# A Gram matrix matmul of 224 columns instead of 256, and one output matmul with an add behind it

## The reference

```
dots = jnp.einsum('bfd,bgd->bfg', bottom_output, bottom_output)
pairs = dots[:, _TRIL_I, _TRIL_J]
x = jnp.concatenate([bottom_mlp_output, pairs, pad], axis=1)     # 128 + 351 + 1
for w, b in ((w0, b0), (w1, b1), (w2, b2), (w3, b3)):            # 1024, 1024, 512, 256
    x = jax.nn.relu(x @ w.T + b)
return x @ w_out.T + b_out
```

## Time and profile before

| | |
|---|---|
| runs, median of three | 570.75 us |
| profiled execution, first to last instruction | 570.2 us |
| time of the profiled execution around its span | not given apart |
| TensorE busy, weight loads busy | 542.0 us (95%), 531.7 us (93%) |
| ScalarE busy | 340.8 us (60%) |
| VectorE busy | 330.0 us (58%) |
| matmuls of the whole program | 4457 |
| one chunk, from one output row to the next | 64.3 us |

### The profile page before, as it was taken

The page is one execution under the profiler, slowest core; times in us unless marked ns, Lnnn a source line. Parts: engine busy times, 40 slices in busy tenths (PEclk is TensorE's granted clock), DMA queues, the critical chain, the costliest instruction groups (busy, mean ns, idle before and its releaser), DMA issues.

```text
span 570.2 us, 13265 instructions
## 1 busy us (share of the span) xinstructions
PE 542.0 (95%) x4457; PEld 531.7 (93%) x4457; DVE 330.0 (58%) x941; ACT 340.8 (60%) x900; POOL 10.8 (2%) x58
## 2 busy tenths in 40 slices
PE   4768799999999999999999999999999999999997
PEld 3667799999999999999999999999999999999996
DVE  3778678727872488427872488427872488425222
ACT  4988479827971499317971499417981399414112
POOL 1500000000000000000000000000000000000000
PEclk9977899999999999999999999999999999999999
DMA  7987324044304141232304131222304131200000
GB/s 222 260 233 223 89 65 117 12 104 124 109 16 119 37 121 47 61 87 78 109 11 112 43 116 53 62 87 77 109 7 111 47 115 56 55 22 1 1 1 0
DMA packets 89898, 47.32 MB, mean 83 GB/s; under 512 B 25851, under 2 KB 88083, under 8 KB 89875
## 3 DMA queue, kind: packets, MB, share of 16 engines
q1 hardware_dynamic: 89874, 47.02, 29.5%
HBM read 41.03 MB, written 5.98 MB: 82 GB/s over the span
## 4 chain that ended last, share of the span: by engine, by line
PE 73%; ACT 12%; DMA 6%; issue 5%; SPq 2%; DVE 0%; ACTq 0%; DVEq 0%
PE acc L551 61%; ACT parts L641 9%; PE gram_ps L518 6%; PE turned_ps L502 5%; DMA rows<-in_r_bottom_output_dram 5%; ACT xt L624 2%; ACT h_full L654 1%; DMA blocks<-grams 1%; PE gram_ps L485 1%; SPq L366 1%; SPq L355 1%; SPq L344 1%; DMA pairs<-blocks 1%; PE turned_ps L564 0%; PE turned_ps L527 0%
## 5 line engine op out<-in xcount | busy, mean ns | idle before, releaser
L551 PE MATMUL acc<-h_a,w_hi 128*128 128x256 f32 x1152 | 211.2, 283 | 0.9 <-ACT h_full L654 0.8
L654 ACT ACTIVATE h_full<-acc,small_t 128x256 f32<-128x256 f32 x176 | 83.2, 473 | 183.2 <-PE acc L551 181.5
L551 PEld LDWEIGHTS acc<-h_a,w_hi 128*128 128x128 f32 x1152 | 179.2, 191 | 2.2 <-ACT h_full L654 2.2
L641 ACT ACTIVATE parts<-gram_ps 27x216 f32<-27x216 f32 x512 | 173.4, 339 | 5.9 <-PE gram_ps L518 1.1
L551 PE MATMUL acc<-h_a,w_lo 128*128 128x256 f32 x576 | 163.0, 283 | 0.0
L551 PEld LDWEIGHTS acc<-h_a,w_lo 128*128 128x128 f32 x576 | 110.4, 192 | 0.0
L551 PE MATMUL acc<-x,w_hi 128*128 128x256 f32 (+1 forms) x512 | 98.5, 289 | 3.7 <-DVE x L806 3.7
L518 PE MATMUL gram_ps<-xt 128*128 128x256 f32 x512 | 95.9, 312 | 1.0 <-ACT parts L641 0.7
L551 PE MATMUL acc<-h_b,w_hi 128*128 128x256 f32 x512 | 93.3, 284 | 0.0
L736 DVE TENSOR_TENSOR xt<-turned_ps,xt 128x432 fp32r<-128x432 f32 x128 | 77.3, 604 | 18.7 <-ACT xt L624 15.7
L502 PE MATMUL turned_ps<-ident,rows 108*128 108x108 f32 x512 | 72.8, 267 | 16.0 <-DMA rows<-in_r_bottom_output_dram 15.1
(11 more groups left out here) (54 smaller groups left out, 346.3 us busy)
## 6 DMA issues: line engine op xcount, KB each, us to landing
rows<-in_r_bottom_output_dram SPq DMA_DIRECT2D x128, 216.0 KB
blocks<-grams SPq DMA_DIRECT2D x32, 182.2 KB
stage_b<-in_L_rec_w_dram SPq DMA_DIRECT2D x2, 1024.0 KB, 9.6
stage_b<-in_L_rec_w_dram SPq DMA_DIRECT2D x1, 2048.0 KB, 7.8
stage_a<-in_L_rec_w_dram SPq DMA_DIRECT2D x1, 1536.0 KB, 11.5
stage_pairs<-in_L_rec_w_dram SPq DMA_DIRECT2D x1, 1408.0 KB, 9.7
mlp_rows<-r_bottom_mlp_output_dram SPq DMA_DIRECT2D x8, 128.0 KB, 2.2
pairs<-blocks SPq DMA_DIRECT2D x8, 126.0 KB
```

The source lines that it names most:

```text
L551: last = nc.tensor.matmul(acc_slot(slot), weight(wp, layer, m, k), in_tile(layer, k, xp), start=(k == 0 and n == 0), stop=(k == K_TILES[la ...
L641: last = nc.scalar.activation(parts[quad, u % 2, :, :, 0:FEATS], gram_ps[quad, b:b + GRAM_BANKS, :].rearrange("p a (b h n) -> p h (a b) n" ...
L654: nc.scalar.activation(h_full[:, slot % 2, :], acc_slot(slot), ACT.Relu, bias=small_t[:, slot:slot + 1]).then_inc(drained, 1)
```

## The change

The Gram matmul streams 28 columns of each sample (27 features and one zero), not 32: 224 columns. The stationary operand stays 128 columns wide. `xt` keeps its layout, so the moving operand is read in eight pieces of 28, and the results stand 28 apart in PSUM. ScalarE's copies L641 take them from there; their number and size stay.

The output row's two accumulating matmuls become one of 512 columns, high and low side by side in the whole bank. ScalarE reads the high half with the bias into `y_row` and gives a new semaphore, out_started. VectorE then adds the low half to `y_row` and gives out_drained.

```diff
+NARROW = 28
+HALF = GROUP * NARROW
...
-        out_bank = turned_ps[0:1, OUT_UNIT % TURN_RING, 0:CHUNK]
+        out_both = turned_ps[0:1, OUT_UNIT % TURN_RING, 0:2 * CHUNK]
+        out_high, out_low = out_both[:, 0:CHUNK], out_both[:, CHUNK:2 * CHUNK]
...
-                    last = nc.tensor.matmul(gram_ps[:, u % GRAM_RING * GRAM_BANKS + j // 2, at:at + 2 * P], xt[:, u % XT_RING, j, 0, :],
-                                            xt[:, u % XT_RING, j].rearrange("p h n -> p (h n)"), start=True, stop=True)
+                    last = nc.tensor.matmul(
+                        gram_ps[:, u % GRAM_RING * GRAM_BANKS + j // 2, at:at + 2 * HALF], xt[:, u % XT_RING, j, 0, :],
+                        xt[:, u % XT_RING, j].rearrange("p h (s f) -> p (h s) f", s=GROUP)[:, :, 0:NARROW],
+                        start=True, stop=True)
...
-                for part in range(2):
-                    last = nc.tensor.matmul(out_bank, ones[:], h_a[:, 4, part, :], start=(part == 0), stop=(part == 1))
-                last.then_inc(out_filled, 1)
+                nc.tensor.matmul(out_both, ones[:], h_a[:, 4].rearrange("p h n -> p (h n)"),
+                                 start=True, stop=True).then_inc(out_filled, 1)
...
-                        gram_ps[quad, b:b + GRAM_BANKS, :].rearrange("p a (b h n) -> p h (a b) n", h=2, n=P)[
-                            :, :, :, QUAD * s:QUAD * s + FEATS], ACT.Copy)
+                        gram_ps[quad, b:b + GRAM_BANKS, :].rearrange("p a (b x) -> p (a b) x", x=2 * P)[
+                            :, :, 0:2 * HALF].rearrange("p j (h n) -> p h j n", n=HALF)[
+                                :, :, :, NARROW * s:NARROW * s + FEATS], ACT.Copy)
...
-                nc.scalar.activation(by_sample(y_row[:, :]), cols(out_bank), ACT.Identity,
-                                     bias=bout[:, :]).then_inc(out_drained, 1)
+                nc.scalar.activation(by_sample(y_row[:, :]), cols(out_high), ACT.Identity,
+                                     bias=bout[:, :]).then_inc(out_started, 1)
...
+            def out_row(c):
+                dve.wait_ge(out_started, c + 1)
+                nc.vector.tensor_tensor(by_sample(y_row[:, :]), cols(out_low), by_sample(y_row[:, :]),
+                                        ALU.add).then_inc(out_drained, 1)
...
+                    elif step[0] == "out" and not (isinstance(c, int) and c == 0):
+                        out_row(c - 1)
...
             chunk(CHUNKS - 1)
+            out_row(CHUNKS - 1)
```

More of the change, by code:

```diff
@@ L284, in dlrm_program @@
         out_filled = sem("out_filled")
+        out_started = sem("out_started")
         out_drained = sem("out_drained")
```

## The result

The changed kernel is slower: 574.56 us in the median of 11 runs (572.83 to 576.73) against 570.75 (11 runs of the kernel before beside it, 569.37 to 572.54). The ratio is 1.0057 with a 95% interval of 1.0042 to 1.0072, so 3.3 us (2.4 to 4.1) are lost; it is not the quotient of the two medians, which lie 3.8 us apart. 574.6 was forecast.

A forecast was written before the change was run, and what follows sets the result against it. TensorE was taken to bound chunk 0, ScalarE's copies most of chunks 1 to 6. Add +4.3 in chunks, +0.7 at the end, Gram -1.1: +3.9 us, forecast 574.6 (572.9 to 576.2; with rivals A, B, C 571.6 to 577.2).

The forecast's parts named there:

- about level: Chunk 2: ScalarE needs 1.82 to 2.29 us a unit against 1.94 for TensorE, and started late.
- only units 14 and 15 come after: Chunks 1 to 6: only 8 Gram matmuls a chunk, behind ScalarE's path, save 10 ns each: 0.48 us in all.
- TensorE as the bound, so all 16 units: 0.64 us: Chunk 0: TensorE bounds, so all 64 Gram matmuls save 10 ns each, 0.64 us.
- At most 11 ns, I take 10: Saving per 224-column Gram matmul from a 120 ns period, limited by the next weight load of about 109 ns.
- D: VectorE add's time, taken as 0.68 us; also a rival: ScalarE not the path in chunks 1 to 6, 569.4, chance 0.08.
- rival B: Output row: the add is dear because its strided read pays too, +5.9 us, 576.6; chance 0.09.
- the 0.9 us: Sign: TensorE's six waits before unit 2's transposes are 0.9 us and name VectorE's new line.
- the other two stops: Sign: waits for h_full grow from 0.35 to about 0.65 us, those before Gram matmuls from 0.2 to about 0.45.
- 0.55 over that span: Whole kernel before: the runs' median, 570.75 us, lies 0.55 over the profiled span of 570.2.
- A: Output row rival: the add is cheap, 0.42 us, since one partition from PSUM hides the stride: 572.8; chance 0.15.
- C: Gram rival: no saving, since the load's handshake is the 120 ns: +5.0 us, 575.7; chance 0.11.
- E: Gram rival: under 256 columns each column costs more, 72 ns more per matmul, about 604 us; chance 0.07.

The follow-up runs named there:

- narrow: Kernel before with only the Gram matmul cut to 224 columns, output row as before: 569.55 us against 570.52, ratio 0.9996.
- narrow3: Kernel before with 224-column Gram matmuls and only three of four Gram copies per unit on ScalarE: 560.65 us, ratio 0.9827.
- wide3: Kernel before, 256 columns, but ScalarE makes only three of the four Gram copies of each unit: 563.72 us, ratio 0.9897.
- cols128: Kernel before with Gram matmuls streaming, and ScalarE copying, only the 128 columns of the high half: 561.9 us in one execution.
- flat: Changed kernel with y_row read and written at unit step by ScalarE and VectorE: 570.84 us in one execution.
- late_add: Changed kernel with the output row moved behind the chunk's last unit, out of its own buffer: 569.44 us, ratio 0.9986 to the kernel before.
- outrow: Kernel before with only the output row changed (one 512-column matmul and the VectorE add), Gram matmuls of 256 columns: 575.18 us, ratio 1.0096.

## Why the prediction was right, and where not

- **The bound.** Right for chunks 1 to 6: narrow lost all its saving but 0.03 us to ScalarE's row, narrow3 got 0.54. The two engines were not "about level", though: ScalarE's row of 28.58 us holds 14 rounds of copies, 2.04 us each with all that stands between them, against 1.94 for a unit on TensorE. But "only units 14 and 15 come after", 8 matmuls, was one unit too many: the copies that end near 228.5 are unit 13's, and four matmuls come after them. Wrong for chunk 0, "TensorE as the bound, so all 16 units: 0.64 us". From the first Gram matmul there to the first output matmul it is 53.16 us in both profiles of before, 52.91 and 52.84 after: 0.28 saved. With faster matmuls ScalarE became the path there too, and a new stop of 0.3 us stands before unit 15's Gram matmuls at 104.26; the 0.3 row in the list of waits is this one. With ScalarE's copies cut to three the same stretch goes from 53.16 (wide3) to 52.56 us (narrow3), 0.59 us less, so nearly all that was forecast comes there. A stage in which one engine is only just ahead of the other has room for a part of the gain.
- **Gram matmul.** "At most 11 ns, I take 10": 7 were measured, 119.0 to 112.1. The most frequent distances are 110 and 114, not 109. That the next load is the floor was right (cols128: 112 to 113 ns with 128 columns). The Trainium skill (TensorE: Matmul & The Clock Gate, Back-to-back issue gap) gives 96 ns for 224 columns by its formula, but states this for a single gap and says that in a stream of weight loads and matmuls both set the spacing; the trace agrees with the second and not with the 96.
- **The add.** D was put at 0.68 from the price of a strided write in L763; it was 0.60. Without the step it is 0.405 (0.416 was taken from L800), so the step costs 0.75 ns an element and not 1.08. Read and write in steps cost 0.19 us together, less than the 0.28 that the prediction has for the write by itself: rival B is out. The Trainium skill (SBUF — State Buffer, the note on SBUF cachelines) says that each access that crosses to a new 16-byte line pays; the 0.25 and 0.19 us of flat agree.
- **The path of the add.** As forecast: the stop grew by 0.64 in place of 0.71, six times, and ScalarE's idle time before its row by the same. VectorE had room. Of the signs, the 0.9 us came as 0.85, and the other two stops ("about 0.65" and "about 0.45") as 0.63 and 0.52. At the end of the program the add cost 0.63 (5.52 us from the last layer matmul against 4.89).
- **The sum.** From the two pairs of profiles: 6 x (64.94 - 64.32) = +3.7, -0.28 for chunk 0, +0.63 at the end: +4.0 us, against 3.8 between the medians and 3.3 (2.4 to 4.1) by the ratio. Forecast +3.9. That the forecast meets the median to 0.1 us is luck. Two errors went against each other: the seven stops were 0.07 to 0.08 too dear (0.5 us), and the Gram saving was put at 1.1 us where 0.28 + 6 x 0.03 = 0.5 came, so 0.6 us too much. With either alone the forecast would have been off by 0.5 to 0.6 us, still well inside its band of 572.9 to 576.2.
- **The base.** "0.55 over that span" was a coincidence of a long execution with the median; the true distance is 2.5 us. It did no harm, since the forecast added a difference to the median.
- **Rivals.** A (0.42) is what the add costs without its step, so it was the right number for another kernel. C was near for chunks 1 to 6, for another reason: the saving was there, ScalarE took it. D is out by narrow: ScalarE has no slack but is 0.10 us a unit behind, and only with three copies of four (wide3) does it idle, 0.4 us at a time. E is out: 224 columns take less than 256.

## What to carry to other kernels

Before an instruction is made shorter, ask of each stage which engine runs there without a hole. TensorE at 95%, with two stops of 0.2 to 0.35 us a chunk, was not the path among the units, and a saving of 6% on its Gram matmuls mostly lengthened the stops. A small add put between a result and the semaphore that frees its bank costs its whole length wherever the next writer of the bank already waits; the same add cost nothing inside a chunk where that writer comes well after it (late_add), so look for the place first. Compare repeating stages of two profiles, not their spans.

## What was not expected of the hardware

- A stream of fp32r matmuls with 256 columns starts every 120 ns, with weights of one column (L564) or of 128. With 224 columns, and with 128, most distances are 110 to 114 ns, and the weight loads start 109 to 113 ns apart.
- The waiting VectorE add started 0.09 us before the end of the instruction ahead of it (flat, 195.29 against 195.38).
- ScalarE's row of copies is 28.57 to 28.65 us long from one execution to another, alike in all chunks of one; the cause is open.
- In outrow and late_add the granted clock of TensorE fell at the last output matmul, behind 1.96 us of idle time (0.59 from 568.90 us, 0.60 from 563.40), and the 512 columns took 0.59 and 0.55 us. In the changed kernel, behind the same idle time, it was still 1.00 there, and they took 0.39. What decides between the two is open.
